# Start of a mixing and low-rank adapter kernel: second x tile ahead of the side columns, passes of the first product and ScalarE's first steps in another order

## What is computed

```python
h = gelu(cond @ W0 + b0); h = gelu(h @ W1 + b1)
att = softmax(h @ W2 + b2)
y = einsum('boi,bih->boh', einsum('bk,koi->boi', att, weight), x) + (att @ bias_k)[:, :, None]
base = einsum('bsd,od->bso', y, base_W)
logits = einsum('bsd,ed->bse', y, router_W)          # gate of the two best of 8
mid = einsum('bsd,edr->bser', y, lora_A) * gate[..., None]
out = x + base + einsum('bser,erd->bsd', mid, lora_B) * 2
```

## Time and profile before

| what | us |
|---|---|
| median of 3 runs | 959.52 (959.34 to 960.11) |
| profiled execution, its own time | 959.47 |
| its span | 957.6 |
| TensorE busy | 949.1 (99% of the span) |
| VectorE busy | 741.8 (77%) |
| GpSimd busy | 295.8 (31%) |
| ScalarE busy | 237.8 (25%) |

### The profile page before, as it was taken

One profiled execution on the slowest core, in us unless ns is written; L12 is line 12 of the kernel. 1 busy time (PEld: TensorE's weight loads), 2 busy tenths in 40 slices (PEclk: granted clock), 3 DMA queues, 4 the chain that ended last, 5 costly groups with the idle time before them and its releaser, 6 DMA issues.

```text
span 957.6 us, 17843 instructions
## 1 busy us (share of the span) xinstructions
PE 949.1 (99%) x5777; PEld 876.6 (92%) x5777; DVE 741.8 (77%) x1641; ACT 237.8 (25%) x546; POOL 295.8 (31%) x230
## 2 busy tenths in 40 slices
PE   7999999999999999999999999999999999999998
PEld 6999999999999999999999999999999999999997
DVE  5778877877777877778777778777778777787775
ACT  5444222222212222222222122222222222222220
POOL 3012333123332133332233331333321333312331
PEclk9999999999999999999999999999999999999999
DMA  9766234423234332333332343333343323433311
GB/s 349 202 191 176 80 108 140 133 96 106 99 115 137 110 115 93 104 126 134 110 110 78 115 137 122 102 104 105 115 136 110 114 82 104 137 133 99 110 44 66
DMA packets 47125, 116.04 MB, mean 121 GB/s; under 512 B 20480, under 2 KB 20864, under 8 KB 45952
## 3 DMA queue, kind: packets, MB, share of 16 engines
q1 hardware_dynamic: 46112, 111.41, 35.0%
q0 software_dynamic: 576, 4.19, 2.3%
q10 hardware_dynamic: 416, 0.16, 0.1%
HBM read 77.97 MB, written 33.59 MB: 116 GB/s over the span
## 4 chain that ended last, share of the span: by engine, by line
PE 98%; DMA 1%; SPq 0%; issue 0%; ACT 0%; DVE 0%
PE pc L518 17%; PE pa L529 13%; PE pb L529 13%; PE y_ps L493 12%; PE pb L532 9%; PE pa L532 9%; PE pd L518 9%; PE pd L609 5%; PE pc L609 4%; PE pc L591 1%; PE pd L591 1%; DMA x_sb<-in_x 1%; PE pa L546 1%; PE pb L546 1%; PE pd L599 1%; PE pa L554 1%
## 5 line engine op out<-in xcount | busy, mean ns | idle before, releaser
L493 PE MATMUL y_ps<-mix_w,x_sb 128*128 128x128 f32 x1024 | 193.5, 273 | 1.0 <-DMA x_sb<-in_x 0.9
L409 POOL TENSOR_TENSOR out_sb<-out_sb,u 128x512 f32<-128x512 f32 x90 | 127.8, 1450 | 202.0 <-DVE u L1239 202.0
L493 PEld LDWEIGHTS y_ps<-mix_w,x_sb 128*128 128x128 f32 x1024 | 166.9, 188 | 13.3 <-DMA x_sb<-in_x 1.1
L379 POOL TENSOR_TENSOR ya<-ya 128x512 f32<-128x512 f32 x30 | 40.0, 1334 | 380.2 <-DVE ya L1142 380.2
L1142 DVE TENSOR_TENSOR ya<-y_ps,bias_sb 128x512 f32<-128x512 f32 x128 | 87.8, 686 | 38.3 <-PE y_ps L493 34.7
L518 PE MATMUL pc<-w_hi,s_hi 128*128 128x512 f32 x236 | 97.5, 413 | 0.0
L529 PE MATMUL pa<-w_hi,a_hi 128*128 128x376 f32 x240 | 94.6, 394 | 0.7 <-ACT p L956 0.7
L518 PE MATMUL pc<-w_hi,s_lo 128*128 128x512 f32 x236 | 92.8, 393 | 0.0
L518 PE MATMUL pc<-w_lo,s_hi 128*128 128x512 f32 x236 | 92.2, 391 | 0.0
L941 ACT ACTIVATE exps<-logits,neg_max 128x8 f32<-128x8 f32 x64 | 19.3, 301 | 260.6 <-DVE neg_max L1161 260.6
L948 ACT ACTIVATE mid_hi<-pd 128x128 fp32r<-128x128 f32 x61 | 16.9, 278 | 269.9 <-PE pd L599 269.9
(11 more groups left out here) (236 smaller groups left out, 2561.1 us busy)
## 6 DMA issues: line engine op xcount, KB each, us to landing
x_sb<-in_x SPq DMA_DIRECT2D x64, 512.0 KB, 3.3
out_sb<-in_x SPq DMA_DIRECT2D x64, 512.0 KB, 4.4
out<-out_sb SPq DMA_DIRECT2D x62, 512.0 KB, 2.8
w_raw<-in_base_t SPq DMA_DIRECT2D x5, 1024.0 KB, 12.7
w_raw<-neg POOLq DMA_DIRECT2D x4, 1024.0 KB, 12.7
bias_sb<-bias_rows SPq DMA_DIRECT2D x62, 64.0 KB, 4.9
out<-out_sb SPq DMA_DIRECT2D x3, 256.0 KB, 2.0
w_raw<-in_side SPq DMA_DIRECT2D x1, 544.0 KB, 8.9
```

Source lines behind the costliest of these rows:

```text
L379: nc.gpsimd.tensor_tensor(y_block(0, 1), y_block(0, 1), y_block(0, 0), ALU.subtract).then_inc(s3_set, 1)
L409: nc.gpsimd.tensor_tensor(o, o, u2[:, :], ALU.add).then_inc(done, 1)
L493: mm = nc.tensor.matmul(y_ps[q % 2][:, j * P:(j + 1) * P], x_sb[m][:, c * P:(c + 1) * P], mix_w[m][:, :], start=True, stop=True)
```

## The change

SyncE issues x tile 1 ahead of the side columns:

```diff
             sp.dma_start(x_sb[0][:, :], x_t[0, :, :]).then_inc(x_in[0], 16)
+            sp.dma_start(x_sb[1][:, :], x_t[1, :, :]).then_inc(x_in[1], 16)
             sp.dma_start(w_raw[W_SIDE], side).then_inc(side_in, 16)
-            sp.dma_start(x_sb[1][:, :], x_t[1, :, :]).then_inc(x_in[1], 16)
```

TensorE runs five warming matmuls and not two ahead of the first product, and that product has all heads first and the tails last:

```diff
-            keep_warm(2)
+            keep_warm(5)
...
+                def low_weights(n):
+                    pe.wait_ge(w_lo_set[B11], n + 1)
+                    for j in range(n * HALF // WP, (n + 1) * HALF // WP):
+                        plain_head(*passes[j][1], B11, pa, j)
+
+                for j in range(HALF):
+                    plain_head(*passes[j][0], B11, pa, j)
+                low_weights(0)
+                pe.wait_ge(op_lo_set[A11], 1)
+                for j in range(HALF):
+                    plain_head(*passes[j][2], B11, pa, j)
+                low_weights(1)
                 pe.wait_ge(side_hi_set, 1)
-                for j in range(HALF):
-                    plain_head(*passes[j][0], B11, pa, j)
-                    plain_tail(*passes[j][0], B11, pa, j, 0)
...
+                for n in (0, 2):
+                    for j in range(HALF):
+                        plain_tail(*passes[j][n], B11, pa, j, 0)
                 pe.wait_ge(side_lo_set, 1)
```

ScalarE makes the side columns' high part behind A11's, negates B11 ahead of the bias rows, places the mixing weights ahead of B22's high part and makes the first exponents ahead of B22's negation:

```diff
             place_mix(0, 1)
-            act.wait_ge(side_in, 16)
-            nc.scalar.activation(w_hi[W_SIDE], w_raw[W_SIDE], ACT.Copy).then_inc(side_hi_set, 1)
...
                 first_a11_high(1, op_hi_set[A11])
+                act.wait_ge(side_in, 16)
+                nc.scalar.activation(w_hi[W_SIDE], w_raw[W_SIDE], ACT.Copy).then_inc(side_hi_set, 1)
                 split_a21(0)
...
+                act.wait_ge(a_in, 16)
+                negate(T2, 0, neg_b11_set)
                 keep_biases()
```

VectorE adds the next pair's first bias ahead of B22's low part, and waits for B22's negation half by half:

```diff
-                dve.wait_ge(neg_b22_set, WP)
+                add_bias(1, 0)
                 for n in range(WP):
+                    dve.wait_ge(neg_b22_set, n + 1)
                     take_lo(B22, n)
-                add_bias(1, 0)
```

More of the change, by code:

```diff
@@ L570, in first_product @@
                 pe.wait_ge(w_hi_set[B11], WP)
-                pe.wait_ge(side_hi_set, 1)
+                def low_weights(n):
+                    pe.wait_ge(w_lo_set[B11], n + 1)
+                    for j in range(n * HALF // WP, (n + 1) * HALF // WP):
+                        plain_head(*passes[j][1], B11, pa, j)
                 for j in range(HALF):
                     plain_head(*passes[j][0], B11, pa, j)
-                    plain_tail(*passes[j][0], B11, pa, j, 0)
+                low_weights(0)
                 pe.wait_ge(op_lo_set[A11], 1)
@@ L577, in first_product @@
                     plain_head(*passes[j][2], B11, pa, j)
-                    plain_tail(*passes[j][2], B11, pa, j, 0)
-                for j in range(HALF):
-                    if j % (HALF // WP) == 0:
-                        pe.wait_ge(w_lo_set[B11], j // (HALF // WP) + 1)
-                    plain_head(*passes[j][1], B11, pa, j)
+                low_weights(1)
+                pe.wait_ge(side_hi_set, 1)
+                for n in (0, 2):
+                    for j in range(HALF):
+                        plain_tail(*passes[j][n], B11, pa, j, 0)
                 pe.wait_ge(side_lo_set, 1)
@@ L975, in first_pair @@
                 split_high(A22, 0, y_ready, 4)
-                act.wait_ge(a_in, 16)
-                negate(T2, 0, neg_b11_set)
                 act.wait_ge(c_in, 16)
@@ L981, in first_pair @@
                                          ).then_inc(b12_hi_set, 1)
+                for m in range(2):
+                    place_mix(1, m)
                 act.wait_ge(d_in, 16)
@@ L984, in first_pair @@
                     take_hi(B22, n)
-                for m in range(2):
-                    place_mix(1, m)
+                exponents(0)
                 negate(B22, 1, neg_b22_set)
-                exponents(0)
                 act.wait_ge(lb_in, 16)
```

## The result

| | us |
|---|---|
| changed kernel, median of 18 runs | 960.51 (959.14 to 963.41) |
| kernel before, median of 18 runs beside it | 959.51 (959.31 to 960.11) |
| ratio | 1.0014, 95% interval 1.0008 to 1.0020 |
| forecast | 959.2 (958.2 to 960.1), within 0.2% at 94% |

The median rose by 1.0 us, and its spread from 0.8 us to 4.3: the fastest execution is faster than any of the kernel before, the slowest is nearly 4 us above that kernel's median. The profiled one took 961.63 with a span of 959.8, 2.2 longer than before, so it is one of the slower half.

What follows compares the result with a forecast made beforehand. TensorE was taken to bound the kernel, with only its idle time ahead of about 42 us to win. From 959.47 us, 0.34 won at the mixing weights and 0.03 lost in the first product gave 959.2 (958.2 to 960.1).

Steps and rivals of the forecast that it cites:

- What bounds the kernel, and where a gain can lie: Whole kernel: TensorE is the chain for 98% of the span; only its idle time ahead of about 42 us can be won.
- x ahead of the side columns: Start: TensorE's second mix at about 12.57, 0.70 us sooner; first product may start at 15.08; added warming matmuls cost nothing.
- The low part is late by GpSimd's instruction: First product: A11's low part still comes at 16.76, behind GpSimd's piece; idle stretch of some 0.65, net 0.03 us lost.
- Mixing weights: Next pair's mix: weights ready at 26.5, not 29.95, so TensorE's gap at 29.95 closes; 0.34 us won.
- Sum: Whole kernel: -0.34 + 0.03 = -0.31 us from 959.47, giving 959.2 us.
- the landing of the bias rows: Bias rows written from 20.95, landed at 25.3, loaded at 30.2, at worst 35.3; VectorE's add needs them at 33.6.
- rival two: VectorE's add near 34 us waits for late bias rows: 960.6 us at 7%, slower by over 1.9 us at 3%.

Runs made afterwards that it cites:

- x first alone: Kernel before with only SyncE's order changed, x's second tile ahead of the side columns: 959.38 us, beside 959.43 before.
- the race is taken out: Changed kernel with GpSimd's first adding transfer made to wait until both bias loads of the next pair have landed: 959.19 us.
- VectorE's order back: Changed kernel with VectorE making B22's low part ahead of the next pair's first bias add again: 959.27 us.
- the last version: Changed kernel with VectorE's old order, adding transfer held, B11's low part in four pieces, tails needing no low weights ahead of last low heads: 958.49 us.
- the dose run: Changed kernel with the bias rows' copy and store behind the high parts of A12 and A22: 961.64 us.
- early negation: Kernel before with B11's negation moved ahead of the bias rows, VectorE's order as before: 959.44 us (958.98 to 960.55).

## Why the prediction was wrong

- *What bounds the kernel, and where a gain can lie:* right. All of the difference stands before 44 us.
- *x ahead of the side columns:* right. 12.65 for the forecast 12.57, first product from 15.12 for 15.08, the warming matmuls hidden.
- *The low part is late by GpSimd's instruction:* right, and tested from both sides: x first alone gains nothing, and four pieces free it. The stall was 0.59 for 0.65. The term came out at 0.19 in the profile of the changed kernel, 0.16 of it by GpSimd's later end there, and at 0.06 to 0.08 in five of its relatives (19.59 to 19.61 for 19.53), for the forecast 0.03.
- *Mixing weights:* right. 0.34 forecast; 0.32 in the profile (0.19 behind at 19.7, 0.13 ahead at 30.4), 0.26 between medians in the run that has them alone.
- *Sum:* 959.2 is what the change gives where the race is taken out (959.19, and 959.27 with VectorE's order back).
- *The step that failed is the landing of the bias rows,* "at 30.2, at the worst at 35.3", and with it rival two's chance of 7 and 3%, under "The rivals". The mechanism, its place and its queue were named, and the price per microsecond was right: landing at 36.2 is 2.3 beyond 33.9, and by the forecast's own rule that makes 959.47 - 0.31 + 2.3 = 961.5, where the profiled execution took 961.63. What was wrong is how long the load takes, and how often.

I took its length from all 62 loads, "4.9 in the median and 10.0 at most", although nearly all of them run when no adding transfer does. Those of pairs 1 and 2 were issued shortly before the first two adding transfers had their packets, or while they had them, and in the trace of before these four took 5.8, 10.0, 6.4 and 9.4 us. The maximum itself is one of them: pair 1's second load, issued at 25.2 and landed at 35.2, while the adding transfer's large packets began at 31.5. Only the first load, the one that VectorE's add waits for, was through at 30.5, ahead of them. I wrote that the transfer "now starts ahead of it" and then priced the load as if nothing had changed. "Only the longest load of 62 would do it" was no argument against the rival.

Its terms, as measured: the store took 6.0 us in place of 4.4, the load 9.3 in place of 4.9, landing at 36.2; and, to judge by the tail, something like it happened in two executions of three. The store's 1.6 us are not the collision: it was through at 26.9, ahead of the first large packet, and took 6.3 in the last version, where the transfer is held.

What reading the trace could have given is the packets. The transfer has 128 of 8 KB, eight to each of 16 engines if they are spread evenly, and took 89.6% of the engines for 6 us, so 0.67 us each; a bias load has 256 packets of 256 bytes, 16 to an engine. If a small packet stands behind each of the eight large ones, the load takes 8 x 0.67 = 5.4 us longer than its usual 4.5 to 6.6, which is my estimate from these rows: 9.9 to 12.0. The trace of before had these packets too, at 37 to 41 us.

The Trainium skill (DMA: Bandwidth & Descriptors, section Queues, rings and completion order) says that each DMA engine takes turns between the queues that have work, a packet at a time. By that rule the sum is the one above. The changed kernel's trace agrees: from 28 to 33 us 84 small packets went through beside 112 large ones. The lengths agree within a microsecond: the load took 9.3, 9.6 and 11.7 us where the big transfer led, 4.5 to 6.6 where it didn't. But taking turns is not all of it. With VectorE's order back the load was issued at 26.06, and from 27 to 30 us large packets alone went through, which turns between two queues with work don't give:

```profile
DMA packets 80, 0.66 MB, mean 218 GB/s; under 512 B 0, under 2 KB 0, under 8 KB 0
...
q0 software_dynamic: 80, 0.66, 109.2%
```

What stays open: what holds back the first packets of one of the two when the other is under way (the transfer's where the bias load is issued ahead of it or just behind it, the load's in the rows above), and why 3 of 128 executions of the kernel before were above 960.2 too. Some executions were fast even in the dose run, in whose profile the rows' store was issued 0.5 us behind the transfer.

## What to carry to other kernels

When an edit lets a large transfer start sooner, look for the small-packet transfers that it now meets, and price them by the large packets per engine that can stand in front of theirs, not by their usual time. Look at the spread of the executions too, and not only at the median: the early negation's cost shows in its longest executions, while its median is that of the kernel before. An instruction that waits for such a transfer should stand behind the work that others need, as VectorE's add did before. And where one engine's short instruction stands until another's long one is through, as VectorE's subtraction did behind GpSimd's, cutting the long one in pieces can give more (0.7 us here, with TensorE's order fitted to it) than starting the short one sooner (nothing clear of noise).

## What the runs showed of the hardware

- The first bias load of pair 1, 64 KB in 256-byte pieces, took 4.5 to 6.6 us where an adding transfer of 1 MB came behind it or not at all (6.9 in the dose run, after one), and 9.3 to 11.7 where the transfer's packets led. The 32 KB store took 3.1 to 6.3 us, and 7.7 beside the transfer.
- The adding transfer's first large packet came 1.4 to 1.7 us after its issue, but 2.6 to 6.0 where the bias load had been issued before it or at most 0.39 us after.
- VectorE's subtraction of 512 columns took 0.68 us by itself, and 0.86, 0.98, 1.18, 1.34, 1.53, 1.66 to 1.68 and 1.80 beside GpSimd's subtraction of 1024-column pieces, the longer the sooner it was issued; each time it ended 0.54 to 0.56 us behind GpSimd's end.
- In a stall of 3.3 us TensorE's granted clock fell to its lower level (0.50) and stayed there for some seven microseconds, six of them with work. In the profile with stalls of 0.7 and 1.1 us it stayed full. I hadn't counted this among a stall's costs.
